# Last batch's slots one attention group earlier, its output product in two parts, first expert weights issued later, half sums at the head of a slot

## What is computed

```python
xn = _layernorm(x, axis=-1)
x = x + attn(xn, Wq, Wkv, Wo, bo) + ffn(xn, gate_w, bias, Wg, Wu, Wd, Sg, Su, Sd)
# attn: 32 heads of 16 features, 8 key/value groups, causal softmax, then ctx @ Wo + bo
scores = jax.nn.sigmoid(x @ gate_w.T) + bias
topk_w, topk_idx = jax.lax.top_k(scores, 4)
# normalised weights cw; 16 experts with 256 inner features
out = jnp.einsum('eti,ehi->th', silu(g) * u * cw, Wd)
out = out + (silu(x @ Sg.T) * (x @ Su.T)) @ Sd.T      # the shared expert
```

## Time and profile before

| | us |
|---|---|
| median of 3 runs | 535.72 (535.19 to 537.13) |
| the profiled execution | 536.95 |
| its span in the trace | 535.1 |
| busy PE / PEld | 462.7 / 345.7 |
| busy DVE / ACT / POOL | 361.4 / 283.4 / 235.5 |
| mean granted TensorE clock | 0.952 of full speed |

### The profile page before, as it was taken

How to read it: one execution, slowest core, us unless ns; L and a number is a source line. 1 busy time by engine, 2 the same in 40 slices (tenths; PEclk the granted TensorE clock), 3 DMA queues, 4 the chain that set the end, 5 groups by cost and what they waited for, 6 DMA issues and landing times.

```text
span 535.1 us, 9881 instructions
## 1 busy us (share of the span) xinstructions
PE 462.7 (86%) x3074; PEld 345.7 (65%) x3074; DVE 361.4 (68%) x604; ACT 283.4 (53%) x434; POOL 235.5 (44%) x175
## 2 busy tenths in 40 slices
PE   3998959967999998899985989998969999989870
PEld 2867748845776776667663767676747767767640
DVE  7488644785577868938799595489685655965620
ACT  2722221614656776646786647286726546666610
POOL 2111619631444644634338654152566443264321
PEclk9999979998999998999998789998979999999996
DMA  7916962549746547965777766857674423445243
GB/s 275 375 36 153 249 202 70 148 140 213 211 81 159 116 84 236 244 174 122 151 209 205 218 153 116 213 108 169 181 171 73 83 45 60 78 67 96 42 56 43
DMA packets 31878, 77.93 MB, mean 146 GB/s; under 512 B 4048, under 2 KB 11728, under 8 KB 28912
## 3 DMA queue, kind: packets, MB, share of 16 engines
q1 hardware_dynamic: 18864, 45.92, 27.9%
q0 software_dynamic: 11856, 27.27, 27.8%
q10 hardware_dynamic: 1104, 4.06, 3.7%
HBM read 54.04 MB, written 23.07 MB: 144 GB/s over the span
## 4 chain that ended last, share of the span: by engine, by line
PE 48%; DMA 17%; DVE 15%; issue 7%; ACT 5%; SPq 2%; ACTq 1%; POOL 1%; DVEq 1%; POOLq 0%
PE psum L1173 17%; PE psum L1163 9%; DMA out<-ysb,tab 9%; DVE wsplit L986 6%; DMA q_parts<-stage 4%; PE psum L1315 3%; PE psum L1193 2%; PE psum L1126 2%; DVE plo L1028 2%; PE psum L1214 2%; PE psum L1303 2%; PE psum L1198 2%; PE psum L1181 2%; ACT wsplit L627 1%; PE psum L1280 1%
## 5 line engine op out<-in xcount | busy, mean ns | idle before, releaser
L1173 PE MATMUL psum<-wsplit,xgT 128*128 x564 | 163.0, 429 | 17.7 <-DVE wsplit L986 17.7
L488 POOL DMA_INDIRECT out<-ysb,tab x47 | 81.4, 1732 | 158.1 <-ACT ysb L652 91.7
L1173 PEld LDWEIGHTS psum<-wsplit,xgT 128*128 128x128 f32 x564 | 106.3, 202 | 38.7 <-issue 20.6
L1163 PE MATMUL psum<-wsplit,zT 128*128 (+1 forms) x330 | 90.3, 409 | 7.6 <-DVE zT L957 3.5
L971 DVE TENSOR_REDUCE negm<-psum 128x4 f32<-128x512 f32 x64 | 59.6, 954 | 25.1 <-PE psum L1198 25.1
L478 POOL DMA_INDIRECT xg<-xn_rows,tab x47 | 62.9, 1338 | 29.5 <-PE psum L1214 14.3
L1163 PEld LDWEIGHTS psum<-wsplit,zT 128*128 128x128 f32 x330 | 59.3, 189 | 23.5 <-issue 12.5
L652 ACT ACTIVATE ysb<-psum,tab 128x512 f32<-128x512 f32 x47 | 32.3, 687 | 74.5 <-PE psum L1163 69.2
L1028 DVE TENSOR_TENSOR plo<-xn,phi 128x1536 f16<-128x1536 f32 x32 | 59.1, 1847 | 15.0 <-ACT phi L705 12.9
L981 DVE TENSOR_TENSOR xgT<-psum,xgT 128x512 fp32r<-128x512 f32 x47 | 32.3, 688 | 48.4 <-ACT xgT L623 48.0
L699 ACT ACTIVATE xn<-psum 128x1536 f32<-128x1536 f32 x32 | 46.3, 1446 | 23.0 <-PE psum L1288 14.8
(11 more groups left out here) (190 smaller groups left out, 731.7 us busy)
## 6 DMA issues: line engine op xcount, KB each, us to landing
wraw<-wexp SPq DMA_DIRECT2D x17, 1024.0 KB, 6.6
wraw<-wexp SPq DMA_DIRECT2D x17, 512.0 KB, 4.3
q_parts<-stage SPq DMA_DIRECT2D x16, 192.0 KB
xn<-x SPq DMA_DIRECT2D x4, 512.0 KB, 5.2
xn_rows<-xn SPq DMA_DIRECT2D x8, 256.0 KB, 7.8
ctxs<-x SPq DMA_DIRECT2D x8, 256.0 KB, 4.5
out<-ysb SPq DMA_DIRECT2D x8, 256.0 KB, 3.2
out<-xn POOLq DMA_DIRECT2D x8, 256.0 KB, 4.4
```

The source lines that it names most:

```text
L488: nc.gpsimd.indirect_dma_start(out=out, out_offset=rows_of(s), in_=ysb[:, par, :], in_offset=None, compute_op=ALU.add).then_inc(y_out[par] ...
L1163: last = MM(dst, lhs(a, k), split_weights(place, w, c), start=m == 0, stop=m == len(products) - 1)
L1173: last = MM(bank(GUB[par]), xgT[:, par, a, k, :], split_weights(place, w, k * 512), start=k == 0 and a == w == 0, stop=k == KD - 1 and a = ...
```

## The change

There are four edits.

The diff, without the places in DVE's and PE's loops where only `BESIDE[g]` became `beside(b)[g]` and where the context of a group with a single slot is formed accordingly:

```diff
 BESIDE = ((0, 1), (2,), (3,), (4, 5), (6,), (7, 8), (9,), (10, 11))
+BESIDE_LAST = ((0, 1), (2, 3), (4,), (5, 6), (7,), (8, 9), (10,), (11,))
 SPS = sum(len(s) for s in BESIDE)
...
+        def beside(b):
+            return BESIDE_LAST if b == B - 1 else BESIDE
+
         def arrivals(e):
...
         ZB, NM = 3, 2
-        WO = (PV, 2)
+        WO = (2, 3)
+        EARLY_K, LATE_K = range(KD - 1), range(KD - 1, KD)
         TRB = (0, 1, GU, XT)
...
             pack_half(sp, 1, 0)
-            for part, cols in enumerate(PARTS):
-                sp.dma_start(wraw[:, 0, cols], wexp[0, :, cols]).then_inc(we_in[part][0], 16)
-
-            sp.wait_ge(ws_low, len(STEPS))
-            for part, cols in enumerate(PARTS):
-                sp.dma_start(wraw[:, 1, cols], wexp[1, :, cols]).then_inc(we_in[part][1], 16)
-
             for t in range(NT):
...
                 sp.dma_start(out[t * P:(t + 1) * P, :], ysb[:, t % 2, :]).then_inc(stored[t % 2], 16)
-                if t < 2:
-                    sp.wait_ge(we_in[t][0], 16)
-                    sp.sem_inc(w_ready[t], 1)
+                if t == 1:
+                    for part, cols in enumerate(PARTS):
+                        sp.dma_start(wraw[:, 0, cols], wexp[0, :, cols]).then_inc(we_in[part][0], 16)
+                if t == 3:
+                    sp.wait_ge(ws_low, len(STEPS))
+                    for part, cols in enumerate(PARTS):
+                        sp.dma_start(wraw[:, 1, cols], wexp[1, :, cols]).then_inc(we_in[part][1], 16)
+                        sp.wait_ge(we_in[part][0], 16)
+                        sp.sem_inc(w_ready[part], 1)
...
                 pool.wait_ge(y_out[1 - par], 16 + (16 * ((s - 1) // 2 + 1) if s else 0))
-                if s > SPS and s % SPS in (2, 3):
-                    pool.wait_ge(att_out, 32 * (s // SPS) + (0 if s % SPS == 2 else 16))
+                if s > SPS and s % SPS in (1, 2):
+                    pool.wait_ge(att_out, 32 * (s // SPS) + (0 if s % SPS == 1 else 16))
                 nc.gpsimd.indirect_dma_start(out=out, out_offset=rows_of(s), in_=ysb[:, par, :], in_offset=None,
...
                 pool.wait_ge(att_sb, QT * b + qt + 2)
-                newest = SPS * (b + 1) + 1 + qt if b < B - 1 else NSLOT - 1
+                newest = SPS * (b + 1) + qt if b < B - 1 else NSLOT - 1
                 pool.wait_ge(y_out[newest % 2], 16 + 16 * (newest // 2 + 1))
                 pool.dma_start(out[T * b + P * qt:T * b + P * (qt + 1), :], att[:, qt, :], accum_op=ALU.add).then_inc(att_out, 16)
             def sequence(b, last):
                 for g in range(G):
-                    for j in BESIDE[g]:
+                    for j in beside(b)[g]:
                         if not (last and j + 3 >= SPS - 1):
                             gather(SPS * b + (j + 3), 1 - j % 2, SPS * b + (j + 2))
+                        if b and j in (3, 4):
+                            add_attention(b - 1, j - 3)
                         s = SPS * b + j
...
                             down_low_of(number)
-                        if b and j in (3, 4):
-                            add_attention(b - 1, j - 3)
                 if last:
...
-            def context_evac(b, qt, source):
-                    act.wait_ge(ct_ps, QT * b + qt + 1)
-                    S(ctxT[:, qt, :, :], bank(source).rearrange("p (k n) -> p k n", k=KD), ACT.Copy).then_inc(ct_sb, 1)
+            def context_evac(b, qt, source, chunks=slice(0, KD), late=0):
+                act.wait_ge(ct_ps, QT * (b + late) + qt + 1)
+                S(ctxT[:, qt, chunks, :], bank(source).rearrange("p (k n) -> p k n", k=KD)[:, chunks, :],
+                  ACT.Copy).then_inc(ct_sb, 1)
             def sequence(b, last, ahead):
                 for g in range(G):
-                    for j in BESIDE[g]:
+                    for j in beside(b)[g]:
                         s, par = SPS * b + j, j % 2
                         here, number = ahead
-                        if j == BESIDE[g][0]:
+                        if j == beside(b)[g][0]:
                             numerators(b, g)
-                        if j == BESIDE[g][-1] and (g == 3 or g == 7 and not last):
+                        if j == beside(b)[g][-1] and (g == 3 or g == 7 and not last):
                             minus_maxima(2 * b + (g // 4 + 1), 1 - g // 4)
...
                             context_evac(b - 1, 1, PV)
-                        if j == BESIDE[g][0]:
+                        if last and g == G - 1:
+                            for qt in range(QT):
+                                context_evac(b, qt, qt, slice(0, KD - 1))
+                        if j == beside(b)[g][0]:
                             high16(b, g)
...
                     for qt in range(QT):
-                        context_evac(b, qt, qt)
+                        context_evac(b, qt, qt, slice(KD - 1, KD), 1)
                 return ahead
...
-            def context_transpose(b, qt, to):
-                for k in range(KD):
+            def context_transpose(b, qt, to, chunks=range(KD)):
+                for k in chunks:
                     last = TR(psum[:, to, k * P:(k + 1) * P], ctxs[:, qt, k * P:(k + 1) * P], ident[:, :])
                 last.then_inc(ct_ps, 1)
-            def project_out(b, qt, to):
-                for k in range(KD):
-                    last = MM(bank(to), ctxT[:, qt, k, :], wo_sb[:, k, :], start=k == 0, stop=k == KD - 1)
-                last.then_inc(wo_ps, 1)
-
-            def output_projection(b):
-                pe.wait_ge(ctx_done, G * (b + 1))
-                pe.wait_ge(exp_done, G * (b + 1) + 1)
-                for qt in range(QT):
-                    context_transpose(b, qt, qt)
-                for qt in range(QT):
-                    pe.wait_ge(ct_sb, QT * b + qt + 1)
-                    project_out(b, qt, WO[qt])
+            def project_out(b, qt, to, chunks=range(KD)):
+                for k in chunks:
+                    last = MM(bank(to), ctxT[:, qt, k, :], wo_sb[:, k, :], start=k == 0, stop=k == KD - 1, skip_group_check=True)
+                if KD - 1 in chunks:
+                    last.then_inc(wo_ps, 1)
...
                 for g in range(G):
-                    for j in BESIDE[g]:
-                        s, first, par = s0 + j, j == BESIDE[g][0], j % 2
+                    for j in beside(b)[g]:
+                        s, first, par = s0 + j, j == beside(b)[g][0], j % 2
                         if first:
                             scores(b, g, G * b + (min(g + 4, G) if last else g + 4))
-                        if j == BESIDE[g][-1] and (g == 3 or g == 7 and not last):
+                        if j == beside(b)[g][-1] and (g == 3 or g == 7 and not last):
                             maxima_transpose(G * b + (g + 5), 1 - g // 4)
...
                 if last:
+                    pe.wait_ge(ctx_done, G * b + 6)
+                    pe.wait_ge(exp_done, G * (b + 1) + 1)
+                    for qt in range(QT):
+                        context_transpose(b, qt, qt, EARLY_K)
                     place, number = expert.pop(NSLOT - 1)
                     pe.wait_ge(w_low[1], number)
                     pe.wait_ge(y_sb, NSLOT)
                     down(NT + NSLOT - 1, (NSLOT - 1) % 2, place)
-                if last:
-                    output_projection(b)
+                    for qt in range(QT):
+                        pe.wait_ge(ct_sb, QT * b + qt + 1)
+                        project_out(b, qt, WO[qt], EARLY_K)
+                    weighted(b, G - 1)
+                    pe.wait_ge(ctx_done, G * (b + 1))
+                    for qt in range(QT):
+                        context_transpose(b, qt, qt, LATE_K)
+                    for qt in range(QT):
+                        pe.wait_ge(ct_sb, QT * (b + 1) + qt + 1)
+                        project_out(b, qt, WO[qt], LATE_K)
```

6 lines of the change are left out of this document (3 added, 3 removed).

## The result

The changed kernel takes 531.0 us (median of 20 runs, 526.8 to 536.2), the kernel before 536.2 us in the same comparison. The ratio is 0.9913 with a 95% interval of 0.9887 to 0.9939: 4.7 us (3.3 to 6.1), where 18 us were forecast. The profiled execution of the changed kernel is 532.99 us with a span of 531.2, against 535.1 before.

A forecast was written before the change was run, and what follows sets the result against it. No single engine bounds: a stored unit behind weights, late gathers at batch boundaries, serial row additions at the end. 7.6 + 6 + 3 + 2.3 = 18.9, taken as 18.0 off 536.95, less 1.23: 517.7 us; range 512 to 526.

The forecast's parts named there:

- First weights behind the query units: Near 55 to 75 us, moving expert weights from before a unit's store removes ACT and PE stalls: -7.6 us.
- not kept: Rival: the store still lands late or the second weights meet other stores; 6.35 of 7.6 us lost, 524; chance 0.08.
- Half sums at the head, batch 1: At batch 1's boundary, earlier half sums let POOL's gathers leave sooner, ending PE's gather waits: -6 us, bounds 1.5 and 9.1.
- the price of a link: Time by which one addition into out holds up the next in POOL's chain, taken as about 5.4 us.
- what is late next is DVE: Batch 1, slot 9: with gathers on time, DVE's weights bound PE; product 3.2 us earlier, plus 2.6 for the clock.
- Batch 2: Same pattern as batch 1, smaller: half of 6.1 us taken, -3, bounds 0 and -6.1.
- The last batch: Chain of 12 links at 5.4 us starts one link behind rows +0; final half sums at 520.8, not 523.13: -2.3.
- Slots sooner: zero: Last batch: moving slots a group sooner readies some rows 2 to 4 us earlier but by itself brings about zero.
- +3 if PE's side falls behind the chain: Unfavourable bound of the last batch's -2.3 us: 3 us slower if PE's work lags POOL's additions.
- The split product: End of last batch: twelve of 16 output products run earlier, DVE done at 520.5, hidden by 0.3 us; nothing gained.
- The head placing does nothing: Rival: gathers come as late as now, 9 us of boundary gain vanish, 526 to 527; chance 0.05.
- The collisions: Rival: POOL's weight subtractions meeting DVE operations on SBUF eat the boundary gain, 524 to 527; chance 0.22.

The follow-up runs named there:

- kernel 1: The kernel before with only the later issue of the first two experts' weights; 530.4 us, ratio 0.9882 (0.9831 to 0.9934).
- kernel 7: The changed kernel with each main-loop load of expert weights cut to an eighth, other columns keeping old weights; 530.4 us, ratio 0.9868.
- kernel 6: The kernel before plus the weights' edit, both half sums together at the head of slot 3, and the split output product; 520.6 us, ratio 0.9651.
- kernel 8: The changed kernel with POOL's main-loop subtraction of the down weights cut to an eighth of its columns; 520.5 us, ratio 0.9649.
- kernel 2: The kernel before plus the weights' edit and the half sums at the head, last batch as before; 529.3 us, ratio 0.9857.
- kernel 3: The changed kernel with the last batch's output product whole again, its slots still a group sooner; 531.1 us, ratio 0.9920.
- kernel 4: The changed kernel with the old slot table in the last batch, keeping the split output product; 529.1 us, ratio 0.9871.
- kernel 9: The changed kernel with the down weights' subtraction done whole by DVE at the slot's end instead of by POOL; 520.0 us, ratio 0.9632.

## Why the prediction was wrong

- **First weights behind the query units: right.** -7.6 forecast, 7.2 in the trace at 105 us, 6.3 (3.5 to 9.1) by the ratio of kernel 1. Nothing queued behind the second weights cost anything that showed: the lead at 137.5 us is still 6.8. The rival "not kept" fell.
- **Half sums at the head, batch 1: wrong by all of its 6 us.** Two steps failed. The first is the price of a link. I took 5.4 us everywhere. Rows +0 held the half sum for 7.06 us, not 5.4, with the DMA engines at 0.94 share in 236 to 240, so it left at 240.86, where my 246.1 less the lead of 7.0 is 239.1. And the link that crosses the weight loads stayed long, 7.39 us, where I had shortened it from 6.85 to about 5.7. With that the 4 to 5 us of the gathers' lead are used up; kernel 7 restores them. The second is "what is late next is DVE", priced at a gain of 3.2 us plus 2.6 for the clock. Kernels 6 and 7 have the gathers on time, and batch 1 does not shrink by more than two runs of one program differ (106.9 and 108.8, against 107.9): PE waits for DVE instead, whose operations are stretched where they meet POOL's subtractions. With the subtraction short (kernel 8) it takes 103.9. In the stretch that answers the earlier trace rows, 278 to 288, PEclk is 0.84, not near 1, and PE is busy for 4.97 of 10 us.
- **Batch 2: wrong, -3 forecast, +0.4 to +2.4 found (101.2 before; 103.1, 103.6, 101.6 and 101.8 in the changed kernel and kernels 2 to 4).** The wait for DVE grew from 3.03 to 3.96 us. I had named as open whether POOL's earlier subtraction clears DVE there, and gave it half. It did not clear it.
- **The last batch: wrong in sign, -2.3 forecast, +1.3 in the trace.** The chain of 12 links began where I said, at 450.16, but took 68.7 us (to 518.86), not 65.2. The step that failed first is again the price of a link, 5.4 us each: kernels 2 and 4, which keep the old table, took 69.0 and 67.6 us for the same 12 links, so the 2.3 us are missing there too. Kernel 1, whose last batch is unchanged, takes 74.0 us as well, so +1.3 is inside what this batch varies by, and only the missing gain is shown. What makes the links long with the old table is not shown. "Slots sooner: zero" failed beside it: y of +4 came 4.4 us later behind its predecessor, behind a cast stretched by POOL's subtraction, and rows +4 to +6 waited for y. That is the rival bound "+3 if PE's side falls behind the chain", which I took too lightly; in the medians it is 1.8 to 2.5 us, inside the intervals. The split product was rightly put at nothing.
- **The rivals.** "The head placing does nothing" had 0.05 and was the case, together with the fallen last batch; the reason that I gave against it (the half sum can leave 7.7 us earlier) did not reach the additions behind it. The collisions had 0.22, and their rival contained the mechanism, but as a tax on a gain. It is a cost by itself: 11 us in the medians and 15 by the ratios between the changed kernel and kernel 9 (0.9913 and 0.9632). The Trainium skill (SBUF — State Buffer, "Who interferes with whom") says that a DVE operation with two SBUF inputs and a GpSimd operation that reads SBUF exclude each other; the rows agree, 3.88 us for an operation of 128x256 that takes 0.42 alone. The cast of the row maxima has a single input, and the rows show it stretched too, 3.42 us for 0.18.
- **The sum and the range.** The sum added gains at three places as if each were the only bound there. The low end of the range was not the trouble, but its high end, 526, left out the case in which the first term alone is kept: 536.95 - 7.6 - 1.23 = 528.
